# Loading the score operands in transfers of 32 rows of one side instead of 16 rows of both

## The reference

```python
x = x + attn_a(layernorm(x))   # 16 heads, differential attention: two softmax maps a head
x = x + ffn(layernorm(x))      # weights composed from 32 low-rank factors, gelu
x = x + attn_b(layernorm(x))   # linear attention, elu + 1
x = x + ffn(layernorm(x))
# inside attn_a, for each of the 8 sequences and 16 heads (d = 8):
A1 = Q1 @ K1.T / sqrt(8); A2 = Q2 @ K2.T / sqrt(8)      # causal, 256 x 256
O  = (softmax(A1) - lam * softmax(A2)) @ V              # then RMS norm, * 0.2, @ Wo
```

## Time and profile before

| | us |
|---|---|
| runs | 423.36, 427.91, 429.05 (median 427.91) |
| profiled execution, device time | 427.97 |
| its span, first to last instruction | 426.3 |
| PE busy | 367.6 (86%) |
| DVE busy | 302.6 (71%) |
| ACT busy | 241.2 (57%) |
| POOL busy | 199.1 (47%) |
| DMA queue of SP, share of 16 engines | 37.9% |

### The profile page before, as it was taken

The page is one execution under the profiler, slowest core; times in us unless marked ns, Lnnn a source line. Parts: engine busy times, 40 slices in busy tenths (PEclk is TensorE's granted clock), DMA queues, the critical chain, the costliest instruction groups (busy, mean ns, idle before and its releaser), DMA issues.

```text
span 426.3 us, 10103 instructions
## 1 busy us (share of the span) xinstructions
PE 367.6 (86%) x3380; PEld 238.7 (56%) x3380; DVE 302.6 (71%) x974; ACT 241.2 (57%) x585; POOL 199.1 (47%) x319
## 2 busy tenths in 40 slices
PE   0699895397999888999899798989989989999996
PEld 0566585385555554655455555445866656664774
DVE  6586853068899789797979698785565789998110
ACT  3342341035788778787878687773755243353822
POOL 6224422002458577575858486660026667873000
PEclk9999999599899999999999999999999999999999
DMA  8879999970356425354555500000000000000011
GB/s 208 271 235 336 262 249 237 239 138 2 61 82 90 78 45 77 46 82 66 77 78 78 78 4 3 3 3 1 2 0 2 0 1 2 1 1 2 21 29 49
DMA packets 47347, 34.50 MB, mean 81 GB/s; under 512 B 20033, under 2 KB 41665, under 8 KB 47297
## 3 DMA queue, kind: packets, MB, share of 16 engines
q1 hardware_dynamic: 47296, 33.86, 37.9%
HBM read 25.20 MB, written 8.39 MB: 79 GB/s over the span
## 4 chain that ended last, share of the span: by engine, by line
PE 49%; DVE 17%; issue 9%; SPq 9%; ACT 6%; POOL 5%; DMA 4%; DVEq 0%; POOLq 0%; ACTq 0%
PE ps L1366 6%; PE ps L1157 5%; PE ps L1357 5%; PE ps L1081 4%; SPq L404 3%; ACT arena L823 3%; DVE arena L1499 3%; PE ps L1089 3%; DVE arena L1018 3%; DMA stacks<-arena 3%; PE ps L1076 3%; DVE arena L1512 2%; PE ps L1570 2%; PE ps L641 2%; PE ps L1233 2%
## 5 line engine op out<-in xcount | busy, mean ns | idle before, releaser
L775 POOL TENSOR_SCALAR_AFFINE_SELECT arena<-arena 128x256 f32<-128x256 f32 (+1 forms) x192 | 90.6, 486 | 93.9 <-ACT arena L823 90.1
L823 ACT ACTIVATE arena<-ps 128x512 f32<-128x512 f32 x192 | 109.3, 604 | 28.1 <-PE ps L1115 27.7
L1018 DVE TENSOR_REDUCE arena<-ps 128x4 f32<-128x1024 f32 x64 | 78.3, 1223 | 12.5 <-PE ps L1089 9.8
L1011 DVE CUSTOM_DVE_ANT_0 ps<-ps,future 128x128 f32<-128x128 f32 x256 | 66.3, 321 | 17.1 <-PE ps L1076 17.1
L1440 POOL TENSOR_TENSOR arena<-arena 128x1024 f32<-128x1024 f32 x16 | 34.2, 2136 | 38.8 <-DVE arena L1525 38.8
L1115 PE MATMUL ps<-stacks 50*128 50x256 bf16 x256 | 50.0, 275 | 0.7 <-ACT arena L823 0.7
L1081 PE MATMUL ps<-stacks 48*128 48x256 bf16 x256 | 40.5, 275 | 2.1 <-DVE arena L1018 1.7
L1157 PE MATMUL ps<-arena,values 128*17 128x256 f32 x512 | 40.5, 388 | 0.0
L469 POOL TENSOR_TENSOR qk_parts_sb<-qk_rest,qk_parts_sb 128x512 bf16<-128x512 f32 x16 | 19.1, 1211 | 40.2 <-DVE qk_parts_sb L554 40.2
L1011 DVE DVE_READ_ACCUMULATOR2_ANT arena<- 128x1 f32 x256 | 36.2, 141 | 0.1
L1570 PE MATMUL ps<-arena,upto 128*128 128x384 f32 x96 | 35.9, 486 | 0.0
(11 more groups left out here) (139 smaller groups left out, 735.6 us busy)
## 6 DMA issues: line engine op xcount, KB each, us to landing
stacks<-qk_parts SPq DMA_DIRECT2D x96, 128.0 KB, 4.8
qk_parts<-qk_parts_sb SPq DMA_DIRECT2D x16, 384.0 KB, 5.2
arena<-in_L_ffn_fc_B_dram SPq DMA_DIRECT2D x4, 1024.0 KB, 7.9
arena<-in_L_ffn_fc_A_dram SPq DMA_DIRECT2D x16, 256.0 KB, 5.0
xs<-in_L_attn_a_X_dram SPq DMA_DIRECT2D x4, 256.0 KB, 4.2
qk_parts<-qk_parts_sb SPq DMA_DIRECT2D x8, 128.0 KB, 6.2
stacks<-arena SPq DMA_DIRECT2D x64, 4.0 KB
out_dram<-xs SPq DMA_DIRECT2D x4, 256.0 KB, 2.3
```

Of the source, the lines that this page charges most:

```text
L775: nc.gpsimd.affine_select(out=diag, in_=diag, compare_op=ALU.is_ge, fill=0.0, base=0, pattern=[[0, 2 if s < 2 else UMAPS], [1, P]], channe ...
L823: nc.scalar.activation(probs[:, r, s, :], ps[:, bank, :], ACT.Exp, scale=SCALE).then_inc(exp_done, 1)
L1011: last = nc.vector.tensor_tensor_reduce(out=block, in0=block, in1=future[:], scale=1.0, scalar=LOWEST, op0=ALU.add, op1=ALU.max, accum_out ...
L1018: nc.vector.tensor_reduce(out=rowmax[:, gs, 1, UMAPS * uu:UMAPS * (uu + 1)], in_=ps[:, S_BANK + 1:S_BANK + 3, :].rearrange("p b (m k) -> p ...
```

## The change

`load_stack` still issues six transfers into the same 96 rows of both sides. The order of the first two windows is swapped, on the q and the k side alike, so that the components of the first two windows rise (q: 0 and 0, k: 4 and 5). The first two windows of a half are then one block of 32 rows for each side, loaded by one transfer per half and side; the third window stays as it was, 16 rows and both sides, one transfer per half. Bytes: four transfers of 32 rows x 4 KB and two of 16 rows x 2 sides x 4 KB, 128 KB each, as before. The outermost dimension of the DRAM pattern of the new transfers is the window, of size 2, then 16 rows, then 2048 contiguous elements; the stack's side of it is 32 partitions of 2048 elements.

```diff
-WINDOWS = ((0, 5), (0, 4), (1, 3))
+WINDOWS = ((0, 4), (0, 5), (1, 3))
...
             whole = parts_dram[seq, half]
-            for w, (q_at, k_at) in enumerate(WINDOWS):
-
-                for h in range(2):
-                    src = bass.AP(whole.tensor, whole.offset + q_at * P * SEQ + h * HMAPS * SEQ,
-                                  [[row, 2 * DH], [(k_at - q_at) * P * SEQ, 2], [1, HMAPS * SEQ]])
-                    first = TILE_ROWS * h + 2 * DH * w
-                    eng.dma_start(stacks[first:first + 2 * DH, slot].rearrange("p s m t -> p s (m t)"), src)\
+            both_windows = 4 * DH
+            for h in range(2):
+                for side in range(2):
+                    at, following = WINDOWS[0][side], WINDOWS[1][side]
+                    src = bass.AP(whole.tensor, whole.offset + at * P * SEQ + h * HMAPS * SEQ,
+                                  [[(following - at) * P * SEQ, 2], [row, 2 * DH], [1, HMAPS * SEQ]])
+                    first = TILE_ROWS * h
+                    eng.dma_start(stacks[first:first + both_windows, slot, side].rearrange("p m t -> p (m t)"), src)\
                        .then_inc(stack_in[slot], 16)
+            for h in range(2):
+                q_at, k_at = WINDOWS[2]
+                src = bass.AP(whole.tensor, whole.offset + q_at * P * SEQ + h * HMAPS * SEQ,
+                              [[row, 2 * DH], [(k_at - q_at) * P * SEQ, 2], [1, HMAPS * SEQ]])
+                first = TILE_ROWS * h + both_windows
+                eng.dma_start(stacks[first:first + 2 * DH, slot].rearrange("p s m t -> p s (m t)"), src)\
+                   .then_inc(stack_in[slot], 16)
```

## The result

The changed kernel takes 498.73 us (median, 495.84 to 505.50, 6 runs) against 428.51 us for the kernel before (423.36 to 429.96, 6 runs): ratio 1.1645, 95% interval 1.1591 to 1.1698. It is 70.2 us slower. I had forecast slower, by 27 us, in a range from 436 to 515; the direction held, and so did the number of engines behind it, but the size was 2.6 times too small. The ratios leave out executions more than 1.5% above the fastest of their kernel; of the kernel of experiment 2 that leaves a single one, so it has no ratio.

What follows compares the result with a forecast made beforehand. Transfers were taken to count in two places only, the seam from projection to attention and each group's shift store, both on PE's path. 427.97 + 15.0 (seam) + 11.8 (groups) = 454.8, called 455 us; range 436 to 515.

Steps and rivals of the forecast that it cites:

- Number of engines: Stack loads: the new transfers, with the window of size 2 outermost, run on 2 engines, the same pair each time.
- What a stack costs the pair: Stack load on the two engines: 68 packets x 0.165 us = 11.2 us a stack (10.3 to 12.7), now 5.8.
- W: Time the two engines need for one stack's packets: 11.2 us (10.3 to 12.7).
- The seam: Projection to attention: group 0's shift store waits behind four stacks, slot 6 (first shifted scores) at 116.3 us, +15.0 us.
- The wait for the factors: In the seam, PE's wait for `fc2_A` behind two stacks: 10.8 us more, slot 6 (first shifted scores) at 112.1.
- The groups: Attention groups: shift store behind the load makes periods at least 12.6 us; long ones hide it, short ones add 11.8 us.
- the three short periods in a row at the start: Groups from 112.29 to 142.91 us, mean period 10.2: the first gets 2.3 us, the others about 1.4 and 0.7.
- On 16 engines: Rival for the stack loads: 32 rows written at once, a stack takes 3.9 instead of 5.8 us; 424 us, 11%.
- Dearer packets: Rival for the stack loads: two engines, packets of 0.19 to 0.3 us; 474 to 590 us, 15%, 4% beyond.

Runs made afterwards that it cites:

- experiment 2: The changed kernel with the new pattern for the lower half of the partitions only, the upper half loaded as before: 454.03 us, median of four.
- experiment 1: The changed kernel with the two windows interleaved row by row, so that 16 stands outermost: 429.23 us, ratio 1.0004.
- experiment 3: The changed kernel with every stack load issued one shift store later, stacks 2 and 3 likewise: 580.21 us, ratio 1.358.
- experiment 4: The changed kernel with the last two quarters of the fc2_A factors loaded ahead of the first stack: 496.37 us, ratio 1.16.
- experiment 7: The changed kernel with 32 matmuls put into PE's stop for the shift store in groups 2, 4, ... 12: 492.78 us, ratio 1.1523.
- experiment 5: The changed kernel with the shift stores on ACT's queue: 505.0 us; control, the kernel before with the same move: 477.21 us.

## Why the prediction was right in kind and wrong in size

- *Number of engines.* Right. The missing completions, 897 for 896 expected, 449 for 448 in experiment 2 and one in experiment 1, and the 51 GB/s while a load runs alone show it. That the outermost dimension decides came out of two counts of completions in the kernel before, 16 and 8. The Trainium skill's rule for it (page "DMA: Bandwidth & Descriptors", section "Why a DMA increments its semaphore by 16 and not by 1") holds here at 2 as well.
- *What a stack costs the pair* (W). The packet was right, 0.161 against 0.165 us, but W is 12.0 (experiment 3), not 11.2, and what lies around it 2.5 us and not 1.7: from a load's issue to the waiting engine's start 14.5 us instead of 12.9. I multiplied packets by their best time, which gives 10.9 us at 0.161. In the load issued at 197.32 the first packet on each of the two engines took 0.65 us and those that met the third window on the other engines (202.5 to 204.2) 0.36 to 0.53; there W was 12.6.
- *The seam.* The right step decided it, the shift store behind four stacks (experiment 4), 23.2 us instead of 15.0. The term mis-sized was the price of a stack over what it cost before. I had 11.2 - 5.8 = 5.4 us; by the packets above the four took 48.7 us together, where they had taken 20.3, so 7.1 each: in this part a stack had taken 5 us before and not 5.8, and now it took 12.2 and not 11.2. Four times the missing 1.7 us, and 1.2 us instead of 0.7 from the last packet to PE's start, are 7.3 of the missing 8.2. SP's issues stretch as well (6.90 us over two stores from 75.19 on), but that is not a cause of its own: in the trace there is no gap of more than 0.15 us between 58 and 123.3 us with fewer than two packets in flight, and the 10.45 us over the eight factor transfers were 11.92 in the kernel before. The wait for the factors grew by 7.1 us and not by 10.8, behind a wait of 5.45 us for stack 0 that I had not foreseen; the later wait for the shift store covers both.
- *The groups.* This is the step that failed: 11.8 us forecast, some 46 measured, 40.4 of them up to the last load. Its form was right in the main: a stop behind every second load, none behind the others. Only the three short periods in a row at the start, for which I had three stops, have become a pair like the others, with one stop of 7.0 us. Mis-sized was first the stop, 1.85 us forecast and 5.8 measured, six of them 35.5 us: the shift store landed 16.0 us after the load's issue (197.32 to 213.3), where I had 12.9. That is 1.4 us to the first packet instead of 1.0, 12.6 for the load instead of 11.2, and 1.9 to the landing instead of 0.7. A stop is a difference of two near numbers, 12.6 and 10.75, so that an error of a quarter in the first makes it some three times as long. Missing altogether was the clock: I had written that a lower clock costs nothing in the seam and did not carry the question to the groups. There each stop is followed by a group at 0.72, 2.9 us a pair; experiment 7 shows that it is the clock.
- *Rivals.* "On 16 engines" did not happen, but its price was right when experiment 1 made it happen: a load of 3.9 us. I had put that case at 424; it is 429: PE's wait for the factors shrank only from 10.68 to 9.79 us, and slot 6 started at 102.4, not before 101.3. "Dearer packets" held the measured time in its span (474 to 590) with a wrong mechanism, as the packets were not dearer. That my range reached up to 515, and so over the measured time, I owe to the room left for that rival; this was luck.

## What to carry to other kernels

Before changing the shape of a transfer, count its completions in the trace: they tell how many engines carry it, and an outermost dimension of 2 leaves 14 of 16 idle, while the bytes and the number of transfers look the same. Ask not only whether the slower transfer is in time for its own reader, but what small and urgent transfer stands behind it in the same queue; a part of it on the busy engines is enough to hold up the whole. When a wait is added to an engine that was never idle, price the stop from the difference and then give it a wide range, and add what the clock takes from the work behind it.

## What the runs showed of the hardware

- The granted clock answers to short stops: PE stood 5.8 us after 10.3 us at 1.00, and had 0.72 in the mean over the next 15.4 us, that is some of it at 1.2 and the rest at 2.4 GHz. With 3.65 us of matmuls put into the stop it had 1.00 over whole pairs of periods, in three of five; in the other two PE still stood 2.2 and 2.5 us behind them.
- Four small issues moved to ACT cost 49 us (428 to 477), far more than their own 2.6 us a group: a delay of some 2.3 us a group on the engine that PE waits for, and then 12% more busy time of PE at a clock of 0.89.
- Two engines alone hold 25.5 GB/s each with packets of 4 KB, from DRAM to 32 rows, against 27.2 each in the best slice of all sixteen (435 GB/s).
- In one queue a store of 4 KB spread over 8 engines waited on two of them for a load ahead of it, 5 us, while its other six packets were through at once (206.3 and 211.4 us in the changed kernel). Issued on another engine's queue, its packets on the pair got in between those of the load, 2.6 us after the others (199.3 and 201.9 us in experiment 5).
